# A linear recurrence beside causal attention, from pairs of time steps to blocks of four

## The reference

```python
scores = einsum('bhid,bhjd->bhij', q, k) * scale          # causal softmax branch
y_softmax = softmax(scores + causal_mask) @ v

def step(state, inp):                                     # recurrent branch, over the 4096 tokens
    q_t, k_t, v_t = inp
    state = retention * state + Gamma * (v_t[..., :, None] * k_t[..., None, :])
    y_t = einsum('bhij,bhj->bhi', W_static + state, q_t)
    return state, y_t
y = alpha * y_softmax + (1 - alpha) * y_stp               # alpha: a gate per token and head
```

## Time and profile before

| | |
|---|---|
| runs | 2041.37, 2045.02, 2049.36 us |
| profiled execution, span from first to last instruction | 2045.7 us, granted TensorE clock 0.912 |
| first stage | 0 to about 186 us |
| first maxima of group 0, nothing for ScalarE to do | 186 to 268 us |
| attention and recurrence | 268 to about 1877 us |
| last stage | 1877 to 2046 us |
| busy over the span | TensorE 85%, VectorE 82%, ScalarE 70%, GpSimd 63% |

### The profile page before, as it was taken

The page is one execution under the profiler, slowest core; times in us unless marked ns, Lnnn a source line. Parts: engine busy times, 40 slices in busy tenths (PEclk is TensorE's granted clock), DMA queues, the critical chain, the costliest instruction groups (busy, mean ns, idle before and its releaser), DMA issues. The chain is left out here.

```text
span 2045.7 us, 43648 instructions
## 1 busy us (share of the span) xinstructions
PE 1737.9 (85%) x12880; PEld 609.5 (30%) x12880; DVE 1670.2 (82%) x1904; ACT 1435.6 (70%) x3028; POOL 1282.9 (63%) x1864
## 2 busy tenths in 40 slices
PE   5994588999998999999989999999999998886733
PEld 3441122222333222223332222233322222222622
DVE  4334999999898899998979999989898999531877
ACT  2541068889886879888868898888788888773221
POOL 2002058778784778788828887878266669990536
PEclk9996589999999899999989999999999999977865
DMA  4888132222121422311313223122321112102702
GB/s 129 196 200 187 21 80 65 70 65 86 50 71 52 94 59 69 93 60 54 88 39 90 61 71 91 59 70 74 56 65 58 51 32 77 60 26 71 189 10 73
DMA packets 142269, 159.18 MB, mean 78 GB/s; under 512 B 63184, under 2 KB 90832, under 8 KB 142032
## 3 DMA queue, kind: packets, MB, share of 16 engines
q1 hardware_dynamic: 139648, 154.55, 28.9%
q10 hardware_dynamic: 2384, 1.77, 0.3%
HBM read 117.80 MB, written 38.01 MB: 76 GB/s over the span
## 5 line engine op out<-in xcount | busy, mean ns | idle before, releaser
L1139 ACT ACTIVATE probs<-PS 128x512 f32<-128x512 f32 (+3 forms) x2304 | 1151.0, 565 | 258.3 <-PE PS L1042 189.5
L1186 DVE TENSOR_REDUCE pmax<-PS 128x2 f32<-128x1024 f32 (+3 forms) x1152 | 1232.8, 1123 | 100.2 <-PE PS L1011 83.2
L1042 PE MATMUL PS<-Q_st,K_st 50*128 50x512 f16 (+3 forms) x1408 | 436.4, 371 | 35.0 <-ACT probs L1139 11.3
L950 POOL TENSOR_TENSOR pairs<-pairs,v_exp 128x256 f32<-128x256 f32 x256 | 195.3, 763 | 324.1 <-ACT pairs L1146 322.9
L1011 PE MATMUL PS<-K_st,Q_st 48*128 48x512 f16 (+3 forms) x1408 | 338.6, 365 | 44.6 <-DVE pmax L1186 41.0
L1063 PE MATMUL PS<-probs,V_g 128*17 128x512 f32 (+3 forms) x2816 | 356.2, 580 | 0.0
L942 POOL TENSOR_TENSOR v_exp<-v_exp,k_rows 128x512 f32<-128x512 f32 x256 | 324.4, 1267 | 2.9 <-issue 2.9
L1042 PE MATMUL PS<-Q_st,K_first 50*128 50x512 f16 (+3 forms) x896 | 285.5, 384 | 23.0 <-DVE shift L1201 7.5
L1011 PE MATMUL PS<-K_first,Q_st 48*128 48x512 f16 (+2 forms) x896 | 234.7, 418 | 69.5 <-DVE pmax L1186 49.5
L1223 DVE TENSOR_TENSOR_SCAN two_steps<-retention_sq,pairs 128x257 f32<-128x257 f32 x256 | 241.3, 943 | 51.2 <-POOL pairs L954 51.2
L1042 PEld LDWEIGHTS PS<-Q_st,K_st 50*128 50x128 f16 x1408 | 119.3, 94 | 405.8 <-ACT probs L1139 332.2
(11 more groups left out here) (147 smaller groups left out, 1322.8 us busy)
## 6 DMA issues: line engine op xcount, KB each, us to landing
v_exp<-qkv_t SPq DMA_DIRECT2D x256, 256.0 KB
qkv_t<-proj SPq DMA_DIRECT2D x24, 512.0 KB, 3.7
qk_parts<-parts SPq DMA_DIRECT2D x16, 512.0 KB, 5.4
Q_st<-qk_parts SPq DMA_DIRECT2D x192, 32.0 KB, 3.2
v_rows<-vaug SPq DMA_DIRECT2D x32, 136.0 KB, 6.6
xin<-x SPq DMA_DIRECT2D x8, 512.0 KB, 6.7
k_rows<-qkv_t SPq DMA_DIRECT2D x16, 256.0 KB, 3.9
q_rows<-qkv_t SPq DMA_DIRECT2D x16, 256.0 KB, 4.5
```

Of the source, the lines that this page charges most:

```text
L950: pool.tensor_tensor(pairs[:, n % 2, 1:], pairs[:, n % 2, 1:], v_exp[:, n % RING, 1:CH:2], ALU.add)\
L1042: mm = pe.matmul(PS[:, bank, 0:CH - r * P], keys[rows, pair, kt * P:(kt + 1) * P], Q_st[rows, c, pair, r * P:CH], start=True, stop=(kt < T ...
L1139: act.activation(probs[:, tile % P_SLOTS, h, 0:CH - r * P], PS[:, step[5], 0:CH - r * P], ACT.Exp, scale=SCORE_SCALE).then_inc(exp_done, 1)
L1186: dve.tensor_reduce(pmax[:, s % 2, pair * TPC + j:GH * TPC:PAIRS * TPC, blk], PS[:, bank:bank + SIDES, 0:width], AX.X, ALU.max).then_inc(m ...
```

## The change

A block is now four tokens. With b the block sum of u with its decays, the state at the end of a block is s_end = r^4 s_end(before) + r^3 u_0 + r^2 u_1 + r u_2 + u_3. Four units form a *batch*; a *sweep* is the old burst's 16 units. Per batch:

- GpSimd: four products as before; two additions over two units each (`block_sums`, 512 elements) make pairs; one multiplication by r squared and one addition (512 elements each) make block sums; the carries of four units move in one copy.
- ScalarE: the scaling of the even tokens stays, four a batch. The scaling behind the scan (before: line 1153) is gone.
- VectorE: one scan over 4 x 129 values in place of four over 257. The decays come from a full tile `decay_x`, with a zero in front of each unit.
- GpSimd `weigh`: four products of 516 elements, the block state repeated over four tokens with q, for each unit; the addition for even tokens is gone.
- TensorE: a burst per batch, with the decay inside the block in its weights. Output rows are ordered by the place e of the token in its block: four column groups, e = 0 to 3.
- What the tokens of a block give each other is made apart, once a sweep: GpSimd multiplies k of an earlier token by q of a later one (`lag_products_of`), TensorE sums over j with Gamma and its decay (`lag`, two parts of 384 columns, full width), ScalarE takes both parts out, GpSimd multiplies by v and adds (`lag_values`), and the burst adds the result through `ident`.

The step list changes with it:

```diff
-UNIT_PACE = ((0, 0), (TILES - 9, UNITS))
-LAST_PACE = ((0, 0), (TILE_AT[4], 34), (TILES - 12, UNITS))
+PERIOD = TILES // N_BATCHES          # 9 tiles
+LAST_PERIOD = 8
+SCAN_AT, SCALE_AT, BURST_AT, KQ_AT, LAG_AT = 1, 1, 6, 2, 3
+def recurrence_steps(last):
...
+        for k in range(BATCH):
+            if not (last and B + 2 >= N_BATCHES):
+                add(t + k, "v_load", 0, BATCH * (B + 2) + k)
+            if not (last and B + 1 >= N_BATCHES):
+                add(t + SCALE_AT + k, "scale", 0, BATCH * (B + 1) + k)
+        add(t + SCAN_AT, "scan", 0, B)
+        add(t + BURST_AT, "burst", 0, B)
...
+            add(period * (SWEEP_BATCHES * b - 2) + LAG_AT + part, "lag", 0, b, part)
...
+    def contract(t):                  # called at V
+        for step in recurrence.get(t, ()):
+            if step[0] in ("burst", "lag"):
+                bank = next_bank()
+                steps.append(step + (bank,))
+                evacuations.append((step[0] + "_evac",) + step[1:] + (bank,))
...
                 elif kind == "U":
+                    steps.extend(evacuations)
+                    evacuations.clear()
+                    recurrent(t, ("kq_load", "v_load", "scan", "scale"))
```

The burst on TensorE:

```diff
+                        now = q_rows[:, b % 2, 1:1 + CH].rearrange("p (c e) -> p e c", e=STEP4)
+                        for e in range(STEP4):
+                            pe.matmul(rows(e), static_j[:, half, q * VW:(q + 1) * VW], now[:, e], start=True, stop=False)
+                        for e in range(LAGS):
+                            pe.matmul(rows(e), ident[:, q * VW:(q + 1) * VW], lags[:, b % 2, e * BLOCKS:(e + 1) * BLOCKS],
+                                      start=False, stop=False)
+                        for k in range(BATCH):
+                            own = state[:, B % 2, k]
+                            for e in range(STEP4):
+                                first = 1 + e if e < LAGS else 0
+                                mm = pe.matmul(rows(e), sum_e[:, half, q * BATCH + k, e, :],
+                                               own[:, 1 + e:1 + e + STEP4 * (BLOCKS - 1) + 1:STEP4],
+                                               start=False, stop=(k == BATCH - 1))
```

Products there are 128 tokens wide and read float32 values 16 bytes apart. GpSimd's part:

```diff
+                            pool.tensor_tensor(pairs[:, B % 2, k:k + 2], pairs[:, B % 2, k:k + 2],
+                                               v_exp[:, slot:slot + 2, 1:CH:2], ALU.add).then_inc(pair_made, 1)
...
+                        pool.tensor_tensor(own[:, :, 1:], pairs[:, B % 2, :, 0:PAIR:2],
+                                           decay[:, 1, columns(B)].unsqueeze(2).broadcast_to([P, BATCH, BLOCKS]), ALU.mult)\
...
+                        pool.tensor_tensor(own[:, :, 1:], own[:, :, 1:], pairs[:, B % 2, :, 1:PAIR:2], ALU.add)\
...
+                            pool.tensor_tensor(state[:, B % 2, k].rearrange("p (c e) -> p c e", e=STEP4),
+                                               ends[:, B % 2, k].unsqueeze(2).broadcast_to([P, BLOCKS + 1, STEP4]), q,
+                                               ALU.mult).then_inc(weighed, 1)
```

More of the change, by code:

```diff
@@ L118, in max_item, with add @@
     return pair, side, j, blk, CH if blk < c else (j + 1) * P
[L121 to L126, removed]
+def recurrence_steps(last):
+    period = LAST_PERIOD if last else PERIOD
+    at = {}
+    def add(t, *step):
+        at.setdefault(t, []).append(step)
+    for B in range(N_BATCHES):
+        t = period * B
+        for k in range(BATCH):
[5 more added lines that the diff above has]
+        add(t + BURST_AT, "burst", 0, B)
+    for b in range(1, N_SWEEPS + (0 if last else 1)):
+        add(period * (SWEEP_BATCHES * b - 4) + KQ_AT, "kq_load", 0, b)
+        for part in range(len(LAG_PARTS)):
+            add(period * (SWEEP_BATCHES * b - 2) + LAG_AT + part, "lag", 0, b, part)
+    return at
 def first_steps():
@@ L138, in first_steps @@
             steps.append(release)
+            for part in range(len(LAG_PARTS)):
+                steps += [("lag", 0, 0, part, 2), ("lag_evac", 0, 0, part, 2)]
         if n == MAXES[s] - 1:
@@ L143, in first_steps @@
         steps.append(release)
-    steps.append(("scale", 0, 0))
+    steps += [("scale", 0, n) for n in range(BATCH)]
     return steps
 def group_steps(last):
-    steps, turns, bursts, pending = [], [], [], []
+    steps, turns, pending, evacuations = [], [], [], []
     todo = [(0,) + x for x in ITEMS[AHEAD:]] + ([] if last else [(1,) + x for x in ITEMS[:AHEAD]])
-    used = units = 0
-    decays = []
+    used = 0
+    recurrence = recurrence_steps(last)
     def next_bank():
@@ L181, in values, with recurrent @@
             turns.append([OUT_LEAD, "out_turn", "out_norm", 0, s])
[L183 to L186, removed]
+    def recurrent(t, kinds):
+        for step in recurrence.get(t, ()):
+            if step[0] in kinds:
+                steps.append(step)
+    def contract(t):
+        for step in recurrence.get(t, ()):
+            if step[0] in ("burst", "lag"):
+                bank = next_bank()
+                steps.append(step + (bank,))
+                evacuations.append((step[0] + "_evac",) + step[1:] + (bank,))
     for s in range(NCH):
@@ L205, in group_steps @@
                         values()
[L206 to L209, removed]
+                    contract(t)
                 elif kind == "U":
[L211 to L221, removed]
+                    steps.extend(evacuations)
+                    evacuations.clear()
+                    recurrent(t, ("kq_load", "v_load", "scan", "scale"))
             turn()
             pending.append((s, kt))
-    assert not todo and units == UNITS
+    assert not todo and max(recurrence) < TILES
     values()
-    while bursts:
-        burst()
+    steps.extend(evacuations)
     while turns:
@@ L242, in emptied_before @@
     found, before = {}, dict(tail)
-    counts = {"exp": 0, "turn": 0, "burst": 0}
+    counts = {"exp": 0, "turn": 0, "burst": 0, "lag": 0}
     for x in steps:
@@ L975, in group_units, with columns @@
-                    def group_units(g, last):
-                        for n in range(UNITS):
-                            if not (last and n + 2 >= UNITS):
-                                product(g, n + 2)
-                            if n >= 1:
-                                weigh(g, n - 1)
-                            if not (last and n + 1 >= UNITS):
-                                add_pairs(g, n + 1)
-                        weigh(g, UNITS - 1)
+                    def columns(B):
+                        first = (B // SWEEP_BATCHES % HALF) * HD + B % SWEEP_BATCHES * BATCH
+                        return slice(first, first + BATCH)
@@ new lines, in group_batches @@
+                    def group_batches(g, last):
+                        for B in range(N_BATCHES):
+                            b = B // SWEEP_BATCHES + 1
+                            more = not (last and B + 1 >= N_BATCHES)
+                            more_lags = not (last and b >= N_SWEEPS)
+                            if more:
+                                products(g, B + 1)
+                            weigh(g, B)
+                            if more:
+                                block_sums(g, B + 1)
+                            if B % SWEEP_BATCHES == 1 and more_lags:
+                                lag_products_of(g, b)
+                            if B % SWEEP_BATCHES == 2 and more_lags:
+                                lag_values(g, b)
```

383 lines of the change are left out of this document (238 added, 145 removed).

## The result

The changed kernel takes 2131.55 us (median of four runs, 2120.30 to 2137.39), the kernel before 2044.51 beside it: a ratio of 1.0416, 95% interval 1.0394 to 1.0438. It is slower by 87 us; the forecast was 2058 and the range ended at 2125. The direction held, the size did not.

A forecast was written before the change was run, and what follows sets the result against it. Bound: no full engine but a 2.38 us loop per tile (values, first score, its exponential, fourth score). Bursts +58, lags +33, held-up tiles -76, first stage +2, last stage -4 sum to +13 on 2045.7: forecast 2058 us, range 1985 to 2125.

The forecast's parts named there:

- the burst's work: TensorE's six steps of narrow products per burst: 1.37 us taken, 2.45 kept in case reads 16 bytes apart take twice the time.
- Rival 1: Burst products that step run at half speed or are limited by issue: burst +1.07 us, about 2125 us; 27% with late GpSimd.
- Held bank: Burst's bank, evacuated behind the next tile's first exponential: first to fourth score 1.75 us against 1.08, +0.67 a burst.
- Lags: Two lag parts a sweep on TensorE, 30 in the walked groups: 1.1 us each (0 to 1.65), +33 us.
- Held-up tiles: 168 us of attention in which VectorE, GpSimd or a strip's change holds tiles up: 92 stay, -76 us (-120 to -40).
- Rival 2: VectorE is the real limit of tiles over 2.38 us, so relief counts for more: held-up tiles -123, 1978 us; 28%.
- Plain tile: Attention tile without burst or lag part: carried by the loop, still at 2.38 us after the change.
- scan: VectorE's recurrence, 516 values in one instruction: 1.4 us each, 64 make 90 us, 150 us less work.
- GpSimd: Its work a batch: 17 us, 18 with contention, against 22 available, so it fits.
- VectorE at 82%: VectorE's busy share in attention: expected near 83%, so that it stops being a limit.
- First stage: Before attention: filling `decay_x` on ScalarE takes some 4 to 5 us, partly in its waits, +2 us.
- Last stage: After attention: transfer pieces four times as long, -4 us, between -10 and 0.

The follow-up runs named there:

- b_step16: Kernel before, with only the 16 Gamma products of a burst reading their state values 16 bytes apart: 2107.97 us, ratio 1.0298.
- b_narrow: Kernel before, with each burst product cut into four of 128 columns, read as packed as before: 2046.82 us, ratio 1.0007.
- e_packed: Changed kernel, with the state laid out by place in the block so that TensorE's Gamma products read it packed: 2079.85 us, ratio 1.0171 to the kernel before.
- b_step8: Kernel before, with the Gamma products of a burst reading the state in steps of 8 bytes: 2055.44 us, ratio 1.0057.
- b_step32: Kernel before, with the Gamma products of a burst reading the state in steps of 32 bytes: 2107.09 us, ratio 1.0300.
- e_evac: Changed kernel, with ScalarE emptying burst and lag parts before the next tile's exponentials: 2084.18 us, ratio 1.0178 to the kernel before.
- f_q: Changed kernel with packed state, burst and lag parts evacuated at once, and q copied into packed order once a sweep: 2013.63 us, 0.9830 of the kernel before.
- e_nolag: Changed kernel without lag products, their evacuation and the burst's `ident` products: 2079.08 us, ratio 1.0139 to the kernel before.

## Why the prediction was wrong

**The failed step** is the burst's work: "I take 1.37, by the nearest row in width, and keep 2.45." It is 2.52. The row nearest in width had packed operands, and what decides is the step: 16 bytes apart, float32 operands run at half the rate at 128 and at 512 columns alike (`b_step16`, `b_narrow`, `e_packed`). 64 x (2.52 - 1.37) is 74 us, more than the 60 by which the profiled execution missed (+72.9 against +13). The row that spoke for the step was read (612 against 592 ns at 8 bytes) and weighed as a small cost; `b_step8`, `b_step16` and `b_step32` show a cliff behind it. Rival 1 had the half speed right and the limit by issue wrong. The rule of *Advanced Engine Details and Errata* of the Trainium skill (Memory Cachelines, SBUF Cachelines), two hits to a 16-byte line, is borne out: 8 bytes have two and cost 3%, where the page has full performance, 16 and 32 have one and cost 1.8 times. It was given as making 2.45 the likelier, and then the sum did not follow it.

Term by term:

- *Held bank*: 0.67 forecast, 0.47 measured, -13 us over 64. The mechanism stands (`e_evac`); the fourth score comes 0.30 behind the third, not 0.5, since its bank was already free. With work and hold a typical burst is 2.98 for 2.04, 60 us over 64; by the means all bursts cost 105 more than before (185 over the plain tile, for 79.5), against 58.
- *Lags*: 1.42 each against 1.1, +10. They did not fall where VectorE is behind: the bound of 1.65 was nearer.
- *Held-up tiles*: -86 against -76. Fewer tiles are longer than 2.6 us, 122 of 481 for 224 of 559, and the time over 2.38 falls by 17 to 30 us in each of the four groups, as the forecast's mechanism has it; but no run takes the scans off alone. Two other things are in the number: there are 78 fewer such tiles, at 0.275 each 21 us by themselves, and the clock moved. TensorE's granted clock over attention is 0.96 before and 0.99 after, so it stands at its lower level, 1.2 GHz, for some 127 and 33 us. Of the time over 2.38, 46 of 154 us before and 22 of 68 after lie in tiles mostly at that level. What is cause there and what effect is open. Rival 2's -123 did not come, nor did it in `f_q` (-68).
- *Plain tile* 2.38, *scan* 1.24 (1.4 taken), *GpSimd* in time, VectorE at 82%: as forecast.
- *First stage*: +6.0 for +2, and the two traces understate it. The first reduction of the maxima starts at 186.6 us in the trace of before, but at 179.7 to 182.6 in its six variants, none of which touches this stage; in the changed kernel and its variants it starts at 188.6 to 195.6. The means are 10 us apart. The fill of `decay_x` is one ScalarE instruction of 3.6 us. The larger part is a second read in steps that neither the account of the change nor the sum has: for the new order of the last stage the gate's product takes its weights `gate_t` 16 bytes apart, and eight loads take 1.94 us for 0.97, in eight chunks 7.8 us. No run puts that back alone. Then the first maxima: from the first reduction to the first product with values it is 89.0 us in every run with lags and 85.2 to 85.7 in every run without, `e_nolag` too; VectorE waits 3.19 us there, for maxima behind the first lag parts.
- *Last stage*: +4.5 for -4, but executions of one and the same last stage differ by as much: 171.7 to 176.1 us over the seven traces with the old one, 173.4 to 176.2 over the six with the new. The means are 1 us apart, so the forecast gain of 4 did not come, and a loss is not shown either. The pieces of x and out did get longer (packets under 2 KB fell from 26177 to 17835), those of the softmax branch did not: on the SBUF side they are still 256 bytes, as the transfers of after's last stage (1943 to 2118 us) show, 17835 packets under 512 bytes, in that of before 17985. The start waits 4.16 us on its transfer (4.38 in the earlier trace rows).

The gate's product, the change and its weight loads before and after:

```diff
-    mm = pe.matmul(PS[:, 6, j * H:(j + 1) * H], gate_t[:, par, j * P:(j + 1) * P],
+    mm = pe.matmul(PS[:, 6, j * H:(j + 1) * H], gate_t[:, par, j:CH:TPC],
```

```profile
151.95 0.97 PEld L589 LDWEIGHTS PS<-w_sb,gate_t 128*128 128x128 f32 x8
```

```profile
156.53 1.94 PEld L639 LDWEIGHTS PS<-w_sb,gate_t 128*128 128x128 f32 x8
```

The other rows of these two terms:

```profile
L721 ACT ACTIVATE decay_x<-decay 128x4096 f32<-128x4096 f32 x1 | 3.6, 3607 | 0.0
```

```profile
233.38 5.05 DVE L1329 TENSOR_REDUCE pmax<-PS 128x2 f32<-128x256 f32 x5 [3.19 <-PE PS L1135]
```

```profile
DMA packets 21934, 16.95 MB, mean 97 GB/s; under 512 B 17835, under 2 KB 17835, under 8 KB 21931
```

```profile
1951.40 4.16 DMA stp<-y_stp_t
```

The terms measured in the two traces, 105 + 43 - 86 + 6 + 4.5, make 72.5, against a span longer by 72.9.

## What to carry to other kernels

When a change makes an engine read with a larger step, look for the nearest row in *step*, not in width, and if no row has it, take the dear end: between 8 and 16 bytes the step was a cliff here, and its price multiplies with the count of passes. Look for it wherever the new order is read: here it also stood in the weight loads of the first stage. If a result needs regrouping, let a producer off the critical path write it packed (here GpSimd, 40% dearer by it, in a kernel whose tiles without burst or lag grew by 9 us in all), and take a shared bank out before the work that rotates into it. Work taken off a busy engine gave back only the tiles that it had held up, here 68 to 86 of 263 us; the loop of the plain tile stayed.

## What the runs showed of the hardware

- TensorE, float32 moving operand from SBUF, 512 columns: 592 ns packed, 612 at 8 bytes, 1079 at 16, 1098 at 32; 128 columns with four column groups side by side: a pass of four takes 0.11 us packed, 0.23 at 16 bytes. Weight loads of 128 float32 columns: 192 ns packed, 329 at 16 bytes (medians), 0.12 and 0.24 us from one to the next.
- GpSimd slows too: a product of 516 elements takes 1.11 us with q packed and the state repeated in the inner place, 1.56 with q read 16 bytes apart and the result packed, 1.19 in `f_q` with all packed. *GPSIMD Engine Reference* of the Trainium skill (Performance pitfalls for Q7 kernels) gives half as much again for SBUF reads stepping over more than 8 bytes; the traces have 1.3 times, 1.56 against 1.19, which differ in nothing but how q is read.
- Issue of small products was no limit: 4 start within 20 ns of each other, and 960 more of them cost 2.05 us, 0.07%, with an interval from -0.08% to +0.21% that holds zero.
